# Attention pipeline of a transformer block: another order of the seven stages in a step, and squares before their sums

## The chip, the cores and the metric

The kernel runs on all eight cores of one Trainium2 chip. Each core works on one of the eight sequences, 2048 tokens by 1024 features, with the same program and all weights. The cores exchange nothing. The metric is device time in microseconds of the slowest core.

## The reference

Each sequence goes through a layer norm, and its result `xn` into two paths whose results are added to the input.

```python
xn = _layernorm(x)
x = x + attn_ref(xn) + ffn_ref(xn)

# attn_ref, for 2048 tokens
xi = rmsnorm(xn @ down_w + down_b, norm1_w)           # 1024 -> 512
o1 = branch(xi[..., :256], window=10, shift=5,  ...)  # 8 heads of 32
o2 = branch(xi[..., 256:], window=20, shift=10, ...)
x1 = xn + concat(o1, o2) @ up_w + up_b
out = x1 + gelu(rmsnorm(x1, norm2_w) @ ffn_w1 + ffn_b1) @ ffn_w2 + ffn_b2

# branch: q, k, v from xw @ qkv_w + qkv_b, inside each window
attn = softmax(q * scale @ k.T + bias + mask)
o = (attn @ v) @ pw + pb

# ffn_ref: 8 experts, the two best by a router are weighted in
w = softmax(top-2 logits of silu(t @ rw1 + rb1) @ rw2 + rb2)
y = t + sum_e w[e] * (silu(t @ ew1[e] + eb1[e]) @ ew2[e] + eb2[e])
```

## The kernel before

All is bf16 on TensorE with float32 sums. The program goes through its parts one after the other: layer norm and transposes of x (L304 to L365), the router (L372 to L483), attention (L486 to L857), the up projection with the dense feed-forward part (L859 to L1048), and the eight experts for all tokens (L1051 to L1147), which take the larger half of the time.

Operations are put down by `P.op(engine, builders, rd, wr)` (L50). Each engine gets its instructions in the order in which the calls are made, so the order of the calls is the order of every engine's queue. Dependences are kept by named resources: a reader waits for the writers of its resources, a writer for the earlier readers and also for the earlier writers, its own engine's among them. Two transposes into one PSUM bank by two calls thus run one after the other.

Attention begins with the down projection into XI (L556). Then, for each of four groups of 512 tokens, `xi_sq` (L570) squares the four chunks of XI on VectorE into SQ (L574) and sums each over the partitions by a matmul with ones into the bank PS (L578). ScalarE makes the inverse root of it (L582, L586), a matmul spreads it (L589), and `xi_norm` scales XI on VectorE (L596). SQ is one resource, `rSQ`.

For each of the two branches, queries and keys (L744) and values (L766) of all tokens are computed. Then 17 tiles of 120 tokens (12 windows of 10 or 6 of 20, with a bias tile that shuts out everything outside of a window) go through a software pipeline. `do_tile` (L617) gives seven stages for a tile:

- s0: TensorE, eight score matmuls (L629) into four banks of PF, heads h and h + 4 in one bank; VectorE adds the bias into Z (L635).
- s1: VectorE, negative maximum (L644), and its addition to Z (L649).
- s2: ScalarE, exponential from Z into E (L654).
- s3: VectorE, sum (L658), reciprocal (L661), and scaling of E (L666).
- s4: TensorE, eight transposes of E (L672) into a bank of PBF; ScalarE copies them into PTS (L677).
- s5: TensorE, eight matmuls with the values (L687), all into one bank; ScalarE copies two halves into AVS (L694).
- s6: TensorE, four matmuls of the projection (L705); ScalarE adds its bias into UPIN (L715) twice.

The loop at L791 runs over 23 steps. In step k, stage s of tile k - s is issued, so a step holds seven stages of seven different tiles; the first steps and the last have fewer. Z and E have four buffers, PBF, PTS and AVS two. The four score banks exist once, so s0 of a tile waits until L635 of the tile before has read them. The order within a step is written out: s4, s5, s6, s0, s1, s2, s3. A small tile of 10 tokens for the window at the end of the shifted sequence goes through the same stages without a pipeline (L850).

The loads of the weights of the dense part (L880, L882) wait for the end of attention.

Of the kernel before, what the change touches and what calls it, by code (L numbers as in the profile page):

```python
# [211 lines left out]
def build_nc():  # L212
# [276 lines left out]
    if True:  # L489
# [20 lines left out]
        SQ = esA.enter_context(nc.sbuf_tensor("SQ", [128, 4 * 512], BF16))  # L510
# [13 lines left out]
        if True:  # L524
# [24 lines left out]
            if True:  # L549
                rPA, rPB, rPC, rPS = rPF[0], rPF[1], rPF[2], rPF[3]  # L550
                pbanks = [(PA, rPA), (PB, rPB)]
                for nt in range(NNT):
                    for m in range(4):
                        ps, rps = pbanks[m % 2]
                        blds = [
                            (lambda m=m, nt=nt, k=k, ps=ps: t_.matmul(  # L556
                                ps[:, 0:512],
                                WDOWN[:, 512 * k + 128 * m: 512 * k + 128 * m + 128],
                                XN3[:, k, 512 * nt: 512 * nt + 512],
                                start=(k == 0), stop=(k == 7)))  # L560
                            for k in range(8)]
                        P.op("tensor", blds, rd=[rWDOWN, rXN4[nt]], wr=[rps])
                        P.op("scalar", (lambda m=m, nt=nt, ps=ps: s_.activation(
                            XI3[:, m, 512 * nt: 512 * nt + 512], ps[:, 0:512],
                            AF.Identity, bias=CS["dbc"][:, m: m + 1])),
                            rd=[rps, rCS["dbc"]], wr=[rXI])
                for c in range(4):
                    P.op("vector", (lambda c=c: v_.memset(XI3[:, c, 2048:2052], 0.0)),
                         wr=[rXI])
                def xi_sq(nt):  # L570
                    sl = 1024 * (nt % 2)
                    for c in range(4):
                        sq = SQ[:, sl + 512 * (c % 2): sl + 512 * (c % 2) + 512]
                        P.op("vector", (lambda c=c, nt=nt, sq=sq: v_.tensor_tensor(  # L574
                            sq, XI3[:, c, 512 * nt: 512 * nt + 512],
                            XI3[:, c, 512 * nt: 512 * nt + 512], ALU.mult)),
                            rd=[rXI], wr=[rSQ])
                        P.op("tensor", (lambda c=c, sq=sq: t_.matmul(  # L578
                            PS[0:1, 0:512], CS["onesb"][:, 0:1], sq,
                            start=(c == 0), stop=(c == 3))),  # L580
                            rd=[rSQ, rCS["onesb"]], wr=[rPS])
                    P.op("scalar", (lambda nt=nt: s_.activation(  # L582
                        RSTD[0:1, 0:512], PS[0:1, 0:512], AF.Ln,
                        bias=CS["epsc"][0:1, 1:2], scale=1.0 / 512)),
                        rd=[rPS, rCS["epsc"]], wr=[rRSTD])
                    P.op("scalar", (lambda: s_.activation(  # L586
                        RSTD[0:1, 0:512], RSTD[0:1, 0:512], AF.Exp, scale=-0.5)),
                        rd=[rRSTD], wr=[rRSTD])
                    P.op("tensor", (lambda: t_.matmul(  # L589
                        PC[:, 0:512], CS["onesf"][0:1, 0:128], RSTD[0:1, 0:512],  # L590
                        start=True, stop=True)),
                        rd=[rRSTD, rCS["onesf"]], wr=[rPC])

                def xi_norm(nt):
                    for c in range(4):
                        P.op("vector", (lambda c=c, nt=nt: v_.scalar_tensor_tensor(  # L596
                            XI3[:, c, 512 * nt: 512 * nt + 512], PC[:, 0:512],
                            CS["n1c"][:, c: c + 1],
                            XI3[:, c, 512 * nt: 512 * nt + 512], ALU.mult, ALU.mult)),
                            rd=[rPC, rCS["n1c"], rXI], wr=[rXI])  # L600

                for nt in range(NNT):
                    xi_sq(nt)
                    xi_norm(nt)
                P.replay(blk)
# [4 lines left out]
            if True:  # L610
# [112 lines left out]
                for br in range(2):  # L723
# [65 lines left out]
                                      WPJ, rWPJ, PBc, rPBc))  # L789
                    NSTG = 7  # L790
                    for step in range(17 + NSTG - 1):  # L791
                        for sidx in (4, 5, 6, 0, 1, 2, 3):
                            t = step - sidx
                            if 0 <= t < 17:
                                stages[t][sidx]()
# [381 lines left out]
```

How the kernel before makes its waits and increments, by code:

```python
            def body(eng, queue=list(queue), sems=sems):  # L111
                for waits, builders, semname, amt in queue:
                    for s, v in waits:
                        eng.wait_ge(sems[s], v)
                    for b in builders[:-1]:
                        b()
                    builders[-1]().then_inc(sems[semname], amt)
```

## Time and profile before

| what | value |
|---|---|
| runs | 3140.33 and 3503.17 us, median 3321.75 |
| the profiled execution | 3140.12 us |
| its span (first to last instruction, slowest core) | 3138.6 us |
| spans of the eight cores | 3126.6 to 3138.6 us |
| mean granted TensorE clock | 0.871 to 0.873 |
| TensorE busy | 2569.6 us, 82% |
| VectorE busy | 559.6 us, 18% |
| ScalarE busy | 632.4 us, 20% |
| GpSimd busy | 61.6 us, 2% |
| first L635 of branch one to the last of branch two | 305.6 to 827.7 us |

The span is what the trace covers; the device time has 1.5 us more. PE is TensorE, PEld its weight loads, DVE VectorE, ACT ScalarE, POOL GpSimd. An instruction's busy time runs from its start to its end, and the time in brackets behind a row is how long its engine stood idle before it, and which instruction ended that. The granted clock is a share of 2.4 GHz: 1.00 is the level of 2.4 GHz and 0.50 that of 1.2 GHz.

### The profile page before, as it was taken

How to read it: one execution, taken by the hardware profiler on the slowest of the kernel's cores; microseconds unless marked ns; L12 is line 12 of the kernel's file. 1: busy time of each engine (PE TensorE's matmuls, PEld its weight loads, DVE VectorE, ACT ScalarE, POOL GpSimd, SP SyncE). 2: the span in 40 equal slices, each digit the busy share in tenths (PEclk: the TensorE clock that was granted, in tenths of full speed). 3: DMA queues.
4: the chain of work that ended last, by engine and by line, in shares of the span. 5: the costliest groups of instructions: out<-in, count | busy, mean ns of one | idle time of the engine just before them, and what ended most of it. 6: DMA issues, size and time to landing. Idle time of an engine off the chain costs nothing.

```text
span 3138.6 us, 30438 instructions; the slowest of 8 cores (3126.6 to 3138.6 us)
## 1 busy us (share of the span) xinstructions
PE 2569.6 (82%) x11344; PEld 1119.3 (36%) x11344; DVE 559.6 (18%) x699; ACT 632.4 (20%) x1002; POOL 61.6 (2%) x80
## 2 busy tenths in 40 slices
PE   3764344533468969799999999999999999999999
PEld 1321122221223424334444444444444444444443
DVE  7013434233332130000010010100100001000000
ACT  2222112211211112111212112122121221211222
POOL 0000000000000000100000000000000000000000
PEclk9985555555568969899999999999999999999999
DMA  4220000000060000640420510600700700601201
GB/s 124 28 43 0 0 1 0 1 0 0 0 102 6 1 1 1 97 65 1 67 41 1 88 21 1 108 1 1 108 1 1 108 1 2 107 1 23 59 34 47
DMA packets 65621, 100.92 MB, mean 32 GB/s; under 512 B 4819, under 2 KB 40148, under 8 KB 65484
## 3 DMA queue, kind: packets, MB, share of 16 engines
q0 software_dynamic: 58080, 80.78, 16.9%
q1 hardware_dynamic: 7404, 18.20, 1.8%
q8 instruction: 100, 1.64, 0.2%
q14 instruction: 37, 0.30, 0.0%
HBM read 171.36 MB, written 8.39 MB: 57 GB/s over the span
## 4 chain that ended last, share of the span: by engine, by line
PE 80%; DVE 8%; issue 7%; DMA 2%; ACT 2%; SPq 0%; another core or an unknown queue 0%; DVEq 0%; POOL 0%; ACTq 0%; POOLq 0%
PE PF L1112 29%; PE PF L1093 27%; PE PF L1001 4%; PE PF L976 4%; PE PBF L672 3%; PE PF L687 2%; PE PF L381 2%; DMA WE<-e2w 1%; DVE Z L635 1%; PE PF L629 1%; DVE NEG L644 1%; DVE E L666 1%; PE PBF L918 1%; DVE SUMS L658 1%; PE PF L705 1%
## 5 line engine op out<-in xcount | busy, mean ns | idle before, releaser
L1112 PE MATMUL PF<-WE,EHS 128*128 128x512 bf16 x4096 | 918.6, 380 | 29.6 <-DMA WE<-e2w 10.6
L1093 PE MATMUL PF<-XN,WE 128*128 128x512 bf16 x4096 | 890.9, 379 | 14.4 <-DMA WE<-e1w 13.7
L1100 ACT ACTIVATE EHS<-PF,c_eb1c 128x512 bf16<-128x512 f32 x512 | 351.7, 687 | 1348.9 <-PE PF L1093 1348.7
L1112 PEld LDWEIGHTS PF<-WE,EHS 128*128 128x128 bf16 x4096 | 390.2, 98 | 545.5 <-issue 101.2
L1093 PEld LDWEIGHTS PF<-XN,WE 128*128 128x128 bf16 x4096 | 400.6, 98 | 499.1 <-issue 18.7
L1130 DVE SCALAR_TENSOR_TENSOR S<-PF,WTM,S 128x1024 bf16<-128x1024 f32 x128 | 164.3, 1284 | 1687.4 <-PE PF L1112 1468.5
L672 PE MATMUL PBF<-c_idb,E 120*120 120x120 bf16 (+1 forms) x288 | 90.8, 315 | 223.2 <-DVE E L666 185.6
L672 PEld LDWEIGHTS PBF<-c_idb,E 120*120 120x120 bf16 (+1 forms) x288 | 48.3, 168 | 265.0 <-issue 264.9
L976 PE MATMUL PF<-H,WF 128*128 128x512 bf16 x512 | 122.1, 404 | 6.7 <-ACT MID L983 6.7
L1001 PE MATMUL PF<-WF,MID 128*128 128x512 bf16 x512 | 116.0, 379 | 3.9 <-ACT MID L983 3.9
L687 PE MATMUL PF<-PTS,VT 120*32 120x120 bf16 x272 | 70.9, 260 | 35.7
L677 ACT COPY PTS<-PBF 120x960 bf16<-120x960 bf16 (+1 forms) x36 | 33.0, 917 | 295.8 <-PE PBF L672 295.8
L635 DVE TENSOR_TENSOR Z<-PF,c_bt 120x960 f32<-120x960 f32 x34 | 39.3, 1157 | 255.3 <-PE PF L629 255.3
L976 PEld LDWEIGHTS PF<-H,WF 128*128 128x128 bf16 x512 | 52.1, 103 | 78.2 <-issue 25.1
L342 PE MATMUL PBF<-c_idb,XNT 128*128 128x128 bf16 x128 | 33.8, 264 | 49.5 <-DVE XNT L333 32.8
L381 PE MATMUL PF<-XN,WR 128*128 128x512 bf16 x256 | 56.9, 385 | 20.8 <-DMA WR<-r1w 20.2
L983 ACT ACTIVATE MID<-PF,c_fb1c 128x512 bf16<-128x512 f32 x64 | 44.0, 687 | 133.3 <-PE PF L976 133.0
L1001 PEld LDWEIGHTS PF<-WF,MID 128*128 128x128 bf16 x512 | 47.5, 98 | 65.0 <-issue 12.1
L705 PE MATMUL PF<-AVS,WPJ 128*128 128x120 bf16 (+1 forms) x144 | 30.9, 264 | 42.8 <-ACT AVS L694 31.8
L1085 POOL DMA_DIRECT2D WE<-e2w x32 | 23.9, 756 | 1559.8 <-PE PF L1112 1559.7
L687 PEld LDWEIGHTS PF<-PTS,VT 120*32 120x32 bf16 x272 | 26.9, 99 | 77.2 <-issue 73.7
L629 PE MATMUL PF<-QKV 32*120 32x120 bf16 x272 | 37.5, 334 | 13.9 <-DVE Z L635 10.0
(129 smaller groups left out, 990.6 us busy)
## 6 DMA issues: line engine op xcount, KB each, us to landing
WE<-e1w POOLq DMA_DIRECT2D x32, 1024.0 KB, 38.8
WE<-e2w POOLq DMA_DIRECT2D x32, 1024.0 KB, 19.8
XST<-x SPq DMA_DIRECT2D x16, 512.0 KB, 3.5
out<-OST SPq DMA_DIRECT2D x16, 512.0 KB, 2.6
WF<-f1w POOLq DMA_DIRECT2D x1, 4096.0 KB, 30.4
WF<-f2w POOLq DMA_DIRECT2D x1, 4096.0 KB, 54.1
WR<-r1w POOLq DMA_DIRECT2D x1, 2048.0 KB, 17.5
WDOWN<-dw POOLq DMA_DIRECT2D x1, 1024.0 KB, 12.2
```

Source lines behind the costliest of these rows:

```text
L381: (lambda m=m, nt=nt, k=k, ps=ps: t_.matmul(ps[:, 0:512], WR1[:, 1024 * k + 128 * m: 1024 * k + 128 * m + 128], XN3[:, k, 512 * nt: 512 * ...
L629: P.op("tensor", (lambda h=h, a=a, b=b, nj=nj: t_.matmul(SCP[0:nj, 512 * a + 128 * b: 512 * a + 128 * b + nj], q_ap(h), k_ap(h), start=Tru ...
L635: v_.tensor_tensor(zsl, SCP4[0:nj, :, 0:2, 0:nj], bias_ap, ALU.add)),
L672: P.op("tensor", (lambda j=j: t_.transpose(PT[0:nj, 1024 * p2 + 128 * j: 1024 * p2 + 128 * j + nj], E[0:nj, 960 * p4 + nj * j: 960 * p4 + ...
L687: P.op("tensor", (lambda j=j, h=h, a=a, b=b: t_.matmul(PE2[32 * a: 32 * a + 32, 128 * b: 128 * b + nj], vdst[0:nj, 32 * h: 32 * h + 32], P ...
L705: t_.matmul(PE2[0:128, pcol: pcol + nj], WPJ[:, 256 * kc + 128 * mc: 256 * kc + 128 * mc + 128], AVS[:, 240 * p2 + nj * kc: 240 * p2 + nj ...
L976: (lambda m=m, k=k, ps=ps, hs=hs: t_.matmul(ps[:, 0:512], WF1[:, 2048 * k + 128 * m: 2048 * k + 128 * m + 128], H3[:, k, 512 * hs: 512 * h ...
L1001: blds.append(lambda k=k, h2=h2, tcl=tcl, ph=ph: t_.matmul(ph, MID3[:, k, 128 * tcl: 128 * tcl + 128], WF2[:, 1024 * k + 512 * h2: 1024 * ...
L1093: (lambda m=m, nt=nt, k=k, ps=ps, slot=slot: t_.matmul(ps[:, 0:512], WE13[slot][:, k, 128 * m: 128 * m + 128], XN3[:, k, 512 * nt: 512 * n ...
L1100: P.op("scalar", (lambda e=e, m=m, ps=ps: s_.activation(EHS3[:, m, 0:512], ps[:, 0:512], AF.Silu, bias=CS["eb1c"][:, 16 * e + m: 16 * e + ...
L1112: lambda k=k, h2=h2, tcl=tcl, e=e, PEx=PEx: t_.matmul(PEx[0:128, 512 * h2: 512 * h2 + 512], EHS3[:, k, 128 * tcl: 128 * tcl + 128], WE23[: ...
L1130: P.op("vector", (lambda e=e, tc=tc, PEx=PEx: v_.scalar_tensor_tensor(S[:, 1024 * tc: 1024 * tc + 1024], PEx[0:128, 0:1024], WTM[:, 8 * tc ...
```

## The change

Two places. In `xi_sq` the four squares of a token group get a quarter of SQ each, and all four are issued before the four sum matmuls; before, square and matmul were issued in turn, with two halves of SQ for each parity of the group. In the pipeline the seven stages of a step are issued as s0, s1, s2, s3, s4, s5, s6. No instruction is added or taken away, and none changes its shape.

```diff
                 def xi_sq(nt):
-                    sl = 1024 * (nt % 2)
                     for c in range(4):
-                        sq = SQ[:, sl + 512 * (c % 2): sl + 512 * (c % 2) + 512]
+                        sq = SQ[:, 512 * c: 512 * c + 512]
                         P.op("vector", (lambda c=c, nt=nt, sq=sq: v_.tensor_tensor(
                             sq, XI3[:, c, 512 * nt: 512 * nt + 512],
                             XI3[:, c, 512 * nt: 512 * nt + 512], ALU.mult)),
                             rd=[rXI], wr=[rSQ])
+                    for c in range(4):
+                        sq = SQ[:, 512 * c: 512 * c + 512]
                         P.op("tensor", (lambda c=c, sq=sq: t_.matmul(
                             PS[0:1, 0:512], CS["onesb"][:, 0:1], sq,
                             start=(c == 0), stop=(c == 3))),
@@
                     NSTG = 7
                     for step in range(17 + NSTG - 1):
-                        for sidx in (4, 5, 6, 0, 1, 2, 3):
+                        for sidx in range(NSTG):
                             t = step - sidx
                             if 0 <= t < 17:
                                 stages[t][sidx]()
```

## Rows read from the trace of the kernel before

**Rows 1.** Windows: stretch, its length, busy time (instructions) of each engine, clock, DMA
```profile
460.00:500.00 40.00, 17.06 (x70) 8.48 (x71) 12.76 (x13) 7.14 (x13) 0.00 (x0) 0.50 0.00 0
2000.00:3138.00 1138.00, 1120.86 (x5104) 490.51 (x5101) 102.70 (x80) 232.72 (x331) 22.44 (x28) 1.00 0.23 40
```

**Rows 2.** Waits, 470 to 523 us: total us, times, longest us
```profile
DVE Z L635 <- PE PF L629: 40.8, 4, 10.2
...
PE PBF L672 <- DVE E L666: 19.1, 3, 6.4
```

**Rows 3.** Timeline, one step of branch one: start us, us, instruction, idle before
```profile
471.41 1.16 DVE L635 TENSOR_TENSOR Z<-PF,c_bt 120x960 f32<-120x960 f32 x1 [10.21 <-PE PF L629]
...
473.73 1.16 DVE L649 TENSOR_TENSOR Z<-Z,NEG 120x960 f32<-120x960 f32 x1
...
476.36 1.16 DVE L666 TENSOR_TENSOR E<-E,RCPS 120x960 bf16<-120x960 bf16 x1
...
477.67 1.27 PE L672 MATMUL PBF<-c_idb,E 120*120 120x120 bf16 x3 [6.37 <-DVE E L666]
...
481.24 3.13 PE L687 MATMUL PF<-PTS,VT 120*32 120x120 bf16 x8
...
484.46 0.60 ACT L694 CAST AVS<-PF 128x120 bf16<-128x120 f32 x2 [2.10 <-PE PF L687]
...
486.42 1.20 PE L629 MATMUL PF<-QKV 32*120 32x120 bf16 x8
486.85 0.99 ACT L654 ACTIVATE E<-Z 120x960 bf16<-120x960 f32 x1
...
487.73 1.16 DVE L635 TENSOR_TENSOR Z<-PF,c_bt 120x960 f32<-120x960 f32 x1 [10.21 <-PE PF L629]
```

**Rows 4.** Timeline of VectorE: L635 of tiles 3 and 16, both branches
```profile
315.06 1.15 DVE L635 TENSOR_TENSOR Z<-PF,c_bt 120x960 f32<-120x960 f32 x1
...
520.38 1.16 DVE L635 TENSOR_TENSOR Z<-PF,c_bt 120x960 f32<-120x960 f32 x1 [10.22 <-PE PF L629]
...
622.32 1.15 DVE L635 TENSOR_TENSOR Z<-PF,c_bt 120x960 f32<-120x960 f32 x1
...
827.67 1.16 DVE L635 TENSOR_TENSOR Z<-PF,c_bt 120x960 f32<-120x960 f32 x1 [10.20 <-PE PF L629]
```

**Rows 5.** Timeline and one window of the tails (no s0 left), both branches
```profile
527.58 1.27 PE L672 MATMUL PBF<-c_idb,E 120*120 120x120 bf16 x3
...
527.66 1.16 DVE L649 TENSOR_TENSOR Z<-Z,NEG 120x960 f32<-120x960 f32 x1
...
850.26 1.17 PE L705 MATMUL PF<-AVS,WPJ 128*128 128x120 bf16 x4 [0.95 <-ACT AVS L694]
...
858.95 0.26 PE L705 MATMUL PF<-AVS,WPJ 128*128 128x120 bf16 x1 [0.95 <-ACT AVS L694]
...
857.00:861.00 4.00, 2.16 (x10) 0.98 (x9) 0.00 (x0) 1.24 (x4) 0.00 (x0) 0.50 0.00 0
```

**Rows 6.** Timeline: squares and their sum matmuls, in `xi_sq` and in `a4_sq`, `a4_stats`
```profile
242.97 0.42 DVE L574 TENSOR_TENSOR SQ<-XI 128x512 bf16<-128x512 bf16 x1
...
247.54 0.59 PE L578 MATMUL PF<-SQ,c_onesb 128*1 128x512 bf16 x1 [0.75 <-DVE SQ L574]
...
909.28 4.13 DVE L934 TENSOR_TENSOR H<-MID 128x512 bf16<-128x512 bf16 x8
...
921.97 2.05 PE L942 MATMUL PF<-H,c_onesb 128*1 128x512 bf16 x3
```

**Rows 7.** Timeline and windows: chained transposes at either level of the clock
```profile
909.32 3.34 PE L918 MATMUL PBF<-c_idb,MID 128*128 128x128 bf16 x10 [1.07 <-DVE MID L905]
...
928.15 1.09 PE L918 MATMUL PBF<-c_idb,MID 128*128 128x128 bf16 x3
...
908.00:912.00 4.00, 1.89 (x11) 0.81 (x9) 3.26 (x8) 0.00 (x0) 0.00 (x0) 0.96 1.01 163
...
928.00:932.00 4.00, 2.51 (x12) 1.08 (x11) 0.69 (x1) 1.68 (x3) 0.00 (x0) 0.50 1.08 174
```

## The prediction

> **What bounds the kernel now.** I read the windows by stage first. The expert layers fill TensorE (1120.86 of 1138 us in their last stretch, granted clock 1.00), and nothing in the change touches them. The attention stretch is different: in 40 us TensorE is busy 17.06, VectorE 12.76 and ScalarE 7.14, with the clock at 0.50, the 1.2 GHz level [rows 1]. No engine is full there, so the next view is the waits. In 53 us (a little over three steps of the tile pipeline) VectorE waits four times, up to 10.2 us each, for the score matmuls of L629, and TensorE waits three times, up to 6.4 us each, for the normalised exponentials of L666 [rows 2]. The two take turns.
>
> One step in order of time shows why [rows 3]. VectorE runs a step from the bias add L635 at 471.41 to the end of L666 at 476.36 + 1.16 = 477.52, 6.12 us with the handover. Only then may TensorE start the transposes (stage s4, 477.67), and behind them stand in its queue s5 (481.24), after ScalarE's copies at 484.46 s6, and last s0, the scores of the newest tile (486.42). VectorE's next step starts when these are there, at 487.73. The step is 6.11 + 10.21 = 16.32 us. The scores need nothing of what runs ahead of them: in the order written out at L792 they only stand behind it.
>
> **The change, part by part.** *The stage order.* No instruction is added or removed. On TensorE the same groups follow each other in a circle, but s0 of tile k moves ahead of s4 of tile k-4, which waits for VectorE's step k-1. So the scores for step k are computed while VectorE still works on step k-1, and two half-loops remain, each inside its own engine:
> - VectorE: 6.12 us a step.
> - TensorE: s4, s5, the ScalarE copies inside it, s6, then s0. The first three without any wait for VectorE are seen in the tail of the pipeline, where there is no s0: s6 starts at 850.26 and again at 858.95, 8.69 us [rows 5]. s0 takes 1.20 us (486.42) [rows 3]. Together 9.89 us.
>
> The longer loop sets the step: 9.89 instead of 16.32. The cost of s0 is the choice in it: 1.31 us is the most (until VectorE can start), and 0.14 more if s4 waits behind it as it does now for L666 (477.67 less 477.52); the least is about 0.9, if the next group starts before the last scores have ended. That makes a step 9.6 to 10.15 us; I take 9.89.
>
> Now the count, for a branch. The first four steps have no s4 to s6 and keep their order. L635 of tile 3 starts at 315.06 and of tile 16 at 520.38: 205.3 us; in the second branch 622.32 to 827.67, the same [rows 4]. After the change: steps 4 and 5 are VectorE's, 6.12 each. Tile 6 needs s4 and s5 ahead of its scores: 0.14 + 3.57 (477.67 to 481.24) + 3.13 + 1.31 = 8.15. Then ten steps at 9.89 are 98.9. Sum 119.3, a gain of 86.0. In the tail something is given back: now the s4 of step 17 starts 6.26 us after the last L635 (as 477.67 less 471.41 [rows 3]); after the change it stands behind the s4, s5, s6 of step 16, which run after the last scores, -1.31 + 1.20 + 8.69 = 8.58. The loss is 2.3, the net gain 83.7, for two branches 167.4 us.
>
> What is queued behind each moved instruction: s0 of tile k, now in front, waits for L635 of tile k-1 to have read the score banks. That read ends 1.16 us after VectorE's step k-1 has begun, and TensorE then has 8.69 us of s4 to s6 to do before it comes to this s0; it waits for nothing from step 6 on. s4 of tile k-4 needs L666 of step k-1: 6.12 + 0.14 + 0.11 us after the previous scores, against 9.89, so 3.5 us to spare. On ScalarE the exponential (s2) moves from the last place to the first. It needs the subtraction L649 of the step before, done at 473.73 + 1.16, which is 3.5 us after that step's L635 [rows 3], so it starts as soon as ScalarE is through with s6. It lasts 0.99 us and ends while TensorE is in its s0 and s4, before the copies of s4 and s5 are asked for. ScalarE is busy 7.14 us in 40 now [rows 1], so about 3 us a step, and has 9.9. The stages issue no DMA, and the SyncE and GpSimd queues aren't passed.
>
> *The squares (L573 to L581).* Now square and column-sum matmul alternate, because each square waits for the matmul before it: from the square at 242.97 to the end of the fourth matmul at 247.54 + 0.59 are 5.16 us. After the change four squares run in a row, and then four matmuls. Both kinds still run one behind the other: eight of the same squares elsewhere take 4.13 us, (4.13 - 0.42) / 7 = 0.53 from start to start, and three such matmuls 2.05 us, (2.05 - 0.59) / 2 = 0.73 [rows 6]. All four squares write one resource, so the first matmul waits for the last square: 3 x 0.53 + 0.42 + 0.15 + 3 x 0.73 + 0.59 = 4.94. The gain is 0.2 us a group, 0.9 in four; bounds are 0 (the first group runs partly at the higher clock now) and 2 (squares 0.42 apart). The round trip that goes away was no dearer than the two chains that come: it is cost moved from one place to the other.
>
> The sum is 167.4 + 0.9 = 168.3 us. The work behind attention (the weight loads of L880 and L882 are issued only when attention is through, then the expert layers) moves forward as a block. The span 3138.6 becomes 2970, and with the 1.5 us around it the profiled execution's 3140.1 becomes 2972. The median shown (3321.75) is the mean of 3140.33 and 3503.17; the sum goes by the first, which the profiled execution matches.
>
> **The rivals.** *The clock rises.* TensorE no longer stands still for 6.4 us in each step, so the 2.4 GHz level could be granted. For it: from 908 to 912, where a run of 512-column matmuls ends and transposes begin, the clock is 0.96 [rows 7]. Against it: the tail loop of s4 to s6 with no wait for VectorE, the nearest row to the new loop, stays at 0.50 [rows 5], and so do transposes without a gap [rows 7]. What it would give: chained transposes start (3.34 - 0.26) / 9 = 0.34 us apart at the higher clock and (1.09 - 0.26) / 2 = 0.415 at the lower [rows 7], 0.074 less. Sixteen chained matmuls in s4 and s5 make 1.2 us a step, over twenty full steps and the tails about 34 us: 2938 us. The Trainium skill, TensorE: Matmul & The Clock Gate, section on the HAM clock gate, holds that the engine is throttled by default and activity releases it; read simply, a loop without idle stretches should then reach the higher level, and its section on single matmul latency gives (219 + N) / 1.2 against (398 + N) / 2.4 ns, an estimate of 66 ns less for each chained matmul of 120 columns. By those the time would be about 4 us above this rival's. The tail loop doesn't bear out the first reading.
>
> *A hand-over to ScalarE grows.* If the exponential lands in front of the copies that s6 waits for (L694), it adds up to 0.99 us a step, over twenty steps 20 us: 2992. Against it stands the slack worked out above.
>
> *The loop stays tied.* If another buffer bound s0 of tile k to the end of s3, the step would remain near 16.3 and the time at 3140. The code shows no such resource: scores need the query and key rows, written before the pipeline, and the score banks, free after L635.
>
> *Slower.* VectorE's six operations now run beside TensorE in every step. If they stretched, so that its step became longer than 16.3 us (2.7 times), it would set a longer step than now; at 17 us the time is 3140 + 20 x 0.7 = 3154. Against it: L649 beside running transposes takes 1.16 us [rows 5], as it does alone at 473.73 [rows 3].
>
> **How the numbers follow.** The forecast of 2972 has 0.82; the higher clock 0.07; the dearer ScalarE hand-over 0.07; the tied loop 0.03; slower 0.01. The step's bounds (9.6 to 10.15) make 2966 to 2977. To the first rival below and the second above, with a little for their own sizes, the range is 2935 to 2995; it leaves out less than two in ten, as the sizes of the rivals are themselves uncertain. A measurement can tell about 2% (63 us) from no change. Forecast, clock and hand-over are all faster by more, 0.96; the tied loop is within 2% (0.03); slower 0.01.
>
> **What would show it.** Right: L635's starts are 9.6 to 10.2 us apart in steps 6 to 16 with VectorE's step still 6.1 us; TensorE's wait for L666 is gone from there and VectorE's wait for L629 is under 4 us; the tail steps are unchanged at 8.69; the clock in attention is 0.50; from the first square to the fourth sum matmul about 4.9 us; the expert stretch keeps its length. Wrong: a step above 10.5 with a wait of L694 or L687 for ScalarE (second rival); a clock above 0.6 in attention (first); matmuls of L629 that wait for L666 (third); VectorE operations much longer than 1.2 us (fourth).

## The result and the profile after

| | before | after |
|---|---|---|
| median of all runs | 3255.31 us (10 runs) | 2998.3 us (11 runs) |
| lowest run | 3140.33 us | 2969.3 us |
| the profiled execution | 3140.12 us | 2973.41 us |
| its span | 3138.6 us | 2971.9 us |
| mean granted TensorE clock | 0.871 to 0.873 | 0.892 to 0.895 |

The changed kernel is faster: ratio 0.9457, 95% interval 0.9407 to 0.9508. In some executions of either kernel the cores of one die show a lower TensorE clock than the others and take longer (up to 3506 us before, 3414 us after); the medians in the table contain these, while the ratios and the times of the experiments leave them out.

The expert layers are what they were: their last 1848 us hold the same 8224 weight loads in both traces. The 167 us come from attention, all but about 1 us of them from its pipeline. First one full step of it, from the timeline of the changed kernel (start us, us, engine, line, idle before); all lines behind L574 have one more than before (the squares have one less, L573). In the variants below the numbers shift by a few again, and the operation and its tiles tell which instruction it is.

```profile
383.63 0.77 PE L706 MATMUL PF<-AVS,WPJ 128*128 128x120 bf16 x3 [0.95 <-ACT AVS L695]
...
384.73 1.21 PE L630 MATMUL PF<-QKV 32*120 32x120 bf16 x8
385.16 0.99 ACT L655 ACTIVATE E<-Z 120x960 bf16<-120x960 f32 x1
...
385.87 0.83 PE L673 MATMUL PBF<-c_idb,E 120*120 120x120 bf16 x2
386.05 1.16 DVE L636 TENSOR_TENSOR Z<-PF,c_bt 120x960 f32<-120x960 f32 x1 [3.81 <-PE PF L630]
...
389.47 0.28 PE L688 MATMUL PF<-PTS,VT 120*32 120x120 bf16 x1
...
391.00 1.16 DVE L667 TENSOR_TENSOR E<-E,RCPS 120x960 bf16<-120x960 bf16 x1
...
394.65 1.21 PE L630 MATMUL PF<-QKV 32*120 32x120 bf16 x8
...
395.97 1.16 DVE L636 TENSOR_TENSOR Z<-PF,c_bt 120x960 f32<-120x960 f32 x1 [3.81 <-PE PF L630]
```

A step is 395.97 - 386.05 = 9.92 us; it was 16.32 [rows 3]. The transposes L673 start at 385.87, right behind the scores, where before TensorE stood idle 6.37 us ahead of them until L666 had ended. VectorE now begins its step while they run. It idles 3.81 us in a step instead of 10.21. TensorE no longer waits for VectorE: of its idle time of about 3.3 us a step, 0.95 us are spent on L695, and nearly all of the rest in gaps of about 0.15 us between its own matmuls.

The waits of the changed kernel from 380 to 433 us (total us, times, longest) say the same. The wait of the transposes for the exponentials is no longer in the list, and VectorE's wait for the scores is 3.9 us at most [rows 2].

```profile
ACT PTS L678 <- PE PBF L673: 20.9, 6, 3.5
DVE Z L636 <- PE PF L630: 19.1, 5, 3.9
```

The fill and the end of the pipeline, as starts of VectorE's bias add L636 for tiles 3, 4, 5, 6 and 16 of branch one, and the first transpose behind the last of them and that of the next step, which has no s0:

```profile
316.14 1.15 DVE L636 TENSOR_TENSOR Z<-PF,c_bt 120x960 f32<-120x960 f32 x1
...
322.15 1.15 DVE L636 TENSOR_TENSOR Z<-PF,c_bt 120x960 f32<-120x960 f32 x1
...
328.17 1.15 DVE L636 TENSOR_TENSOR Z<-PF,c_bt 120x960 f32<-120x960 f32 x1
...
336.37 1.16 DVE L636 TENSOR_TENSOR Z<-PF,c_bt 120x960 f32<-120x960 f32 x1 [2.09 <-PE PF L630]
...
435.77 1.16 DVE L636 TENSOR_TENSOR Z<-PF,c_bt 120x960 f32<-120x960 f32 x1 [3.87 <-PE PF L630]
...
444.31 0.32 PE L673 MATMUL PBF<-c_idb,E 120*120 120x120 bf16 x1
...
453.00 0.80 PE L673 MATMUL PBF<-c_idb,E 120*120 120x120 bf16 x2
```

Two steps of 6.0 us, one of 8.2, then ten that sum to 99.4: 119.6 us where there were 205.3 [rows 4].

The clock, by the window of 340 to 430 us in the changed kernel and that of 340 to 380 us in a variant of it (e8_grouped, below). Columns as in [rows 1].

```profile
340.00:430.00 90.00, 58.49 (x254) 29.50 (x253) 52.76 (x55) 28.41 (x55) 0.00 (x0) 0.50 0.00 1
```

```profile
340.00:380.00 40.00, 15.49 (x187) 11.14 (x188) 37.93 (x41) 19.58 (x39) 0.00 (x0) 0.50 0.00 1
```

TensorE is busy 65% of the time now. It was 43% in the window of [rows 1] and 40% over three whole steps (19.49 of 49 us, from 470 to 519 us). Its clock is still at the 1.2 GHz level, and so it is in the variant.

The squares, one token group from the timeline of the changed kernel:

```profile
245.27 2.01 DVE L573 TENSOR_TENSOR SQ<-XI 128x512 bf16<-128x512 bf16 x4
...
247.43 2.05 PE L579 MATMUL PF<-SQ,c_onesb 128*1 128x512 bf16 x3 [5.77 <-DVE SQ L573]
...
249.63 0.58 PE L579 MATMUL PF<-SQ,c_onesb 128*1 128x512 bf16 x1
```

From the first square to the end of the fourth sum are 249.63 + 0.58 - 245.27 = 4.94 us; they were 5.16 [rows 6].

### The profile page after: what moved, and what is told of

Same layout as the page of the kernel before. It is cut to its first block, busy times and chain, and to the rows that moved or that the text cites. A ratio compares the mean times of both kernels' runs of the same rounds, so it can differ in the third digit from the quotient of the medians.

```text
span 2971.9 us, 30248 instructions; the slowest of 8 cores (2961.3 to 2971.9 us)
## 1 busy us (share of the span) xinstructions
PE 2551.1 (86%) x11144; PEld 1118.4 (38%) x11344; DVE 559.1 (19%) x699; ACT 633.0 (21%) x1002; POOL 61.6 (2%) x80
## 4 chain that ended last, share of the span: by engine, by line
PE 83%; issue 7%; DVE 4%; DMA 2%; ACT 2%; another core or an unknown queue 0%; SPq 0%; DVEq 0%; POOL 0%; ACTq 0%; POOLq 0%
PE PF L1113 31%; PE PF L1094 29%; PE PF L1002 4%; PE PF L977 4%; PE PBF L673 3%; PE PF L688 3%; PE PF L381 2%; DMA WE<-e2w 1%; PE PBF L919 1%; PE PF L706 1%; PE PF L630 1%; PE PF L556 1%; DVE H L966 1%; PE PBF L342 1%; PE PF L897 1%
## 5 line engine op out<-in xcount | busy, mean ns | idle before, releaser
L673 PE MATMUL PBF<-c_idb,E 120*120 120x120 bf16 (+1 forms) x288 | 91.4, 317 | 52.8 <-DVE E L667 15.2
L673 PEld LDWEIGHTS PBF<-c_idb,E 120*120 120x120 bf16 (+1 forms) x288 | 48.3, 168 | 93.4 <-issue 90.8
L636 DVE TENSOR_TENSOR Z<-PF,c_bt 120x960 f32<-120x960 f32 x34 | 39.3, 1156 | 84.5 <-PE PF L630 84.5
```

The source lines that it names most:

```text
L673: P.op("tensor", (lambda j=j: t_.transpose(PT[0:nj, 1024 * p2 + 128 * j: 1024 * p2 + 128 * j + nj], E[0:nj, 960 * p4 + nj * j: 960 * p4 + ...
```

## The experiments

The theory to be tested: the step is the longer of two loops (TensorE 9.9 us, VectorE about 6) once s0 no longer stands behind the transposes, and was their sum before. Rivals: the place of ScalarE's exponential carries part of it; the squares do; VectorE is still on the path; TensorE's loop is bound by the matmuls themselves at the lower clock.

**Each part alone.** e1_order_only is the kernel before with the second half of the diff, e2_squares_only with the first half.

> Only the order of the stages changes; squares and sums stay as before. Theory (the order decouples VectorE from TensorE): the step of the 120-token tiles is 9.9 us instead of 16.3, device time about 2974 us, 0.9 us above the whole change, ratio 0.947. Rival (a good part of the gain comes from the squares, because their round trips cost more than the traces' steps say): 2980 us or more, ratio above 0.949.

Measured: 2972.55 us, ratio 0.9438 (0.9353 to 0.9523). The step is 396.70 - 386.79 = 9.91 us.

> Only the squares and their sums change; the order of the stages stays s4, s5, s6, s0, s1, s2, s3. Theory: a token group of this stage takes 12.22 us instead of 12.44, 0.2 us less, and the whole kernel stays at 3139 to 3140 us with steps of 16.3. Rival (as above): 5 us or more are gained in this stage.

Measured: 3137.6 us in one execution, where those of the kernel before beside it began at 3139.65; a token group takes 12.21 us (squares start at 243.47 and 255.68) and the step stays at 16.32. So the order is the whole gain that can be seen in the time. The squares' 0.2 us a group can be read in the trace alone.

**Which move of the order.** The order moves s0 ahead on TensorE, and s2 ahead on ScalarE. Two kernels on the base of the one before part them.

```diff
# e3_s0_first
-                        for sidx in (4, 5, 6, 0, 1, 2, 3):
+                        for sidx in (0, 4, 5, 6, 1, 2, 3):
# e4_exp_first
-                        for sidx in (4, 5, 6, 0, 1, 2, 3):
+                        for sidx in (2, 4, 5, 6, 0, 1, 3):
```

> Base is the kernel before, order s0, s4, s5, s6, s1, s2, s3: TensorE's queue as after the change, but ScalarE's exponential stays last in the step as before. Theory (the place of s0 in TensorE's queue is the whole gain): steps of 9.9 us, device time 2974 us, ratio 0.947. Rival (the gain also needs the exponential ahead of the copies, so that VectorE's sums find it in time): steps above 10.5 us, device time above 2986 us.

> Base is the kernel before, order s2, s4, s5, s6, s0, s1, s3: only ScalarE's exponential moves to the front, TensorE's queue stays as before. Theory: the step stays 16.3 us and the time 3140 us, since no chain runs through the exponential. Rival: if the exponential's place carries part of the gain, the step falls below 16 us.

Measured: 2971.74 us, ratio 0.9438 (0.9353 to 0.9523), for the first and 3140.74 us for the second. VectorE's timeline of e3_s0_first has

```profile
384.10 1.16 DVE L635 TENSOR_TENSOR Z<-PF,c_bt 120x960 f32<-120x960 f32 x1 [3.81 <-PE PF L629]
394.01 1.16 DVE L635 TENSOR_TENSOR Z<-PF,c_bt 120x960 f32<-120x960 f32 x1 [3.80 <-PE PF L629]
```

and that of e4_exp_first

```profile
373.32 1.16 DVE L635 TENSOR_TENSOR Z<-PF,c_bt 120x960 f32<-120x960 f32 x1 [10.20 <-PE PF L629]
...
389.65 1.16 DVE L635 TENSOR_TENSOR Z<-PF,c_bt 120x960 f32<-120x960 f32 x1 [10.21 <-PE PF L629]
```

Steps of 9.91 and 16.33 us. The place of s0 is the whole of it: with s0 in front the step is the same 9.91 us whether the exponential stands first or last, and with s0 behind it stays at 16.3.

**Is VectorE off the path, and from where is it on it again?** Extra additions into a tile that nobody reads stand at the head of s3, two or six of them; the outputs stay as they are.

```diff
                     def s3():
+                        for _ in range(2 if nj == 120 else 0):
+                            P.op("vector", (lambda: v_.tensor_tensor(
+                                PAD[0:120, 0:960], bias_ap, bias_ap, ALU.add)),
+                                rd=rd_bias, wr=[rPAD])
                         P.op("vector", (lambda: v_.reduce_sum(
```

> Base is the changed kernel. Two further VectorE additions of 120x960 into an unused tile stand at the head of s3 of every 120-token tile, ahead of L659, about 2.4 us a step. Theory (two loops side by side, VectorE with 3.8 us to spare in each full step): the step stays 9.9 us; only the two or three steps of the fill that VectorE sets grow, about 5 us a branch, 2983 us in all. Rival (VectorE is still on the path of each step): steps of 12.3 us and about 60 us more, 3035 us.

> Base is the kernel before, with the same two additions at the same place, ahead of L658. Theory (VectorE's six operations and TensorE's four groups stand one behind the other in each step): the additions cost in full, steps of 18.7 us, 14 steps a branch at 2.4, 3207 us. Rival (VectorE's 10.2 us of idle time in a step can take them): steps of 16.3 us and less than 10 us more.

> Base is the changed kernel, six such additions at the head of s3, about 7.4 us a step, which makes VectorE's step about 13.5 us. Theory (the step is the longer of two independent loops): steps of 13.5 us, VectorE without idle time in the full steps, and with fill and tail 65 us more a branch, about 3105 us, still below the kernel before. Rival (one chain through both engines remains): the step is 9.9 + 7.4 = 17.3 us and the time above 3170 us.

Measured: 2979.41, 3204.33 and 3102.71 us. The timeline of VectorE in e5_after_pad2, two steps:

```profile
389.42 1.16 DVE L638 TENSOR_TENSOR Z<-PF,c_bt 120x960 f32<-120x960 f32 x1 [1.48 <-PE PF L632]
392.82 2.41 DVE L662 TENSOR_TENSOR PAD<-c_bt 120x960 f32<-120x960 f32 x2
...
399.34 1.16 DVE L638 TENSOR_TENSOR Z<-PF,c_bt 120x960 f32<-120x960 f32 x1 [1.47 <-PE PF L632]
```

in e6_before_pad2:

```profile
384.51 1.16 DVE L637 TENSOR_TENSOR Z<-PF,c_bt 120x960 f32<-120x960 f32 x1 [10.21 <-PE PF L631]
387.90 2.41 DVE L661 TENSOR_TENSOR PAD<-c_bt 120x960 f32<-120x960 f32 x2
...
403.16 1.16 DVE L637 TENSOR_TENSOR Z<-PF,c_bt 120x960 f32<-120x960 f32 x1 [10.21 <-PE PF L631]
```

and in e7_after_pad6:

```profile
394.52 1.15 DVE L638 TENSOR_TENSOR Z<-PF,c_bt 120x960 f32<-120x960 f32 x1
397.91 7.46 DVE L662 TENSOR_TENSOR PAD<-c_bt 120x960 f32<-120x960 f32 x6
...
407.92 1.15 DVE L638 TENSOR_TENSOR Z<-PF,c_bt 120x960 f32<-120x960 f32 x1
```

The same 2.41 us leave the step at 9.92 in the changed kernel, where they only use up VectorE's idle time (3.81 to 1.48), and make it 18.65 in the kernel before, whose VectorE kept its 10.21 us of idle time in full. With 7.46 us more the step is 13.40, VectorE has no idle time, and TensorE waits 3.44 us in it for the scaling of E (L673 in this kernel). That is a maximum of two loops after the change, a sum before it. The 10 us of idle time that VectorE showed before were no reserve.

**What TensorE's loop is made of.** The theory says that most of it is TensorE waiting for its own matmul, since each `P.op` that writes a bank waits for the last one that wrote it. e8_grouped makes one operation of the eight matmuls of a stage, on the base of the changed kernel: such an operation waits once, at its first matmul, and signals once, at its last. The cut shows s4; s0, s5 and s6 are changed in the same way, s6 in pairs. e9_before_grouped does the same on the kernel before.

```diff
                     def s4():
-                        for j in range(8):
-                            P.op("tensor", (lambda j=j: t_.transpose(
+                        P.op("tensor", [(lambda j=j: t_.transpose(
                                 PT[0:nj, 1024 * p2 + 128 * j: 1024 * p2 + 128 * j + nj],
                                 E[0:nj, 960 * p4 + nj * j: 960 * p4 + nj * j + nj],
-                                CS["idb"][0:nj, 0:nj])),
+                                CS["idb"][0:nj, 0:nj])) for j in range(8)],
                                 rd=[rE[p4], rCS["idb"]], wr=[rPT[p2]])
...
```

> Base is the changed kernel. The eight matmuls of s0, of s4 and of s5 and the pairs of s6 are put down as one operation each, so TensorE no longer waits for its own matmul before the next into the same bank. Nothing is left out. Theory (TensorE's loop of 9.9 us sets the step, and most of it is that waiting): TensorE's loop falls to 5 to 6 us, VectorE's 6.1 us become the bound, steps of 6.1 to 6.3 us, the tail's steps near 5, and 90 to 125 us less in all: 2850 to 2885 us, ratio about 0.91. Rival (the matmuls themselves are the cost, since the clock is at its lower level): steps of 9 us or more and less than 25 us gained, 2950 us.

Measured: 2824.55 us, ratio 0.8997 (0.8979 to 0.9015), 25 us below the range expected. The timeline of TensorE and VectorE in one step of e8_grouped, and s6 in its tail:

```profile
348.99 1.15 DVE L634 TENSOR_TENSOR Z<-PF,c_bt 120x960 f32<-120x960 f32 x1
...
349.22 1.03 PE L670 MATMUL PBF<-c_idb,E 120*120 120x120 bf16 x8 [2.24 <-DVE E L665]
...
350.18 0.40 PE L682 MATMUL PF<-PTS,VT 120*32 120x120 bf16 x8
...
352.05 0.56 PE L700 MATMUL PF<-AVS,WPJ 128*128 128x120 bf16 x4 [1.47 <-ACT AVS L690]
...
352.54 0.46 PE L628 MATMUL PF<-QKV 32*120 32x120 bf16 x8
...
355.01 1.15 DVE L634 TENSOR_TENSOR Z<-PF,c_bt 120x960 f32<-120x960 f32 x1
...
405.19 0.56 PE L700 MATMUL PF<-AVS,WPJ 128*128 128x120 bf16 x4 [1.47 <-ACT AVS L690]
...
408.35 0.56 PE L700 MATMUL PF<-AVS,WPJ 128*128 128x120 bf16 x4 [1.47 <-ACT AVS L690]
```

The step is 6.02 us, VectorE's own, without a gap. TensorE's loop is 3.8 us (349.22 to 352.54 + 0.46), not the 5 to 6 that I had expected: the eight transposes take 1.03 us instead of 3.64, s5 0.40 instead of 3.13, s0 0.46 instead of 1.20, at the same clock of 0.50. So the matmuls themselves were the smaller part of the cost; the larger was that each waited for the one before and its signal. In the tail a step takes 3.16 us (s6 at 405.19 and 408.35), where I had put 5. That is most of the 25 us missing in the expectation: from tile 3 to tile 16 a branch takes 78.3 us instead of 119.6, 83 us in two branches, and of the remaining 66 us 51 lie between the last L635 of the pipeline and that of the small tile (54.21 us in branch one of the changed kernel and 28.57 in e8_grouped, 54.28 and 28.49 in branch two).

> Base is the kernel before (order s4, s5, s6, s0, s1, s2, s3), with the matmuls of s0, s4, s5 and s6 put down as in e8_grouped. Theory (in this order the two half-loops add up, whatever each takes): from the first transpose to the end of the scores TensorE takes 3.8 us in e8_grouped, so the step is 6.0 + 0.2 + 3.8 + 0.1 = 10.1 us, against 6.0 in the other order, and the time 2905 to 2930 us. Rival (once the waits for its own matmuls are gone the order no longer matters): steps near 6 and 2825 us.

Measured: steps of 10.17 us, as the timeline of VectorE on core 4 shows, with 4.05 us of its idle time in each:

```profile
374.64 1.16 DVE L633 TENSOR_TENSOR Z<-PF,c_bt 120x960 f32<-120x960 f32 x1 [4.05 <-PE PF L627]
384.81 1.16 DVE L633 TENSOR_TENSOR Z<-PF,c_bt 120x960 f32<-120x960 f32 x1 [4.05 <-PE PF L627]
```

The time was 2992.37 us, above the expectation, in an execution in which the clock was also lower in stretches without an edit (0.94 instead of 1.00 from 2000 to 2900 us, in the expert layers, on its slowest core, 6). So the kernel ran once more.

> The kernel of e9_before_grouped once more, for its time: in that run the steps were 10.17 us as expected, but the clock was at times lower than usual in stretches that the edit does not touch, on several cores, and the time was 2992 us. Theory (the steps set it): 21 full steps with 4.15 us more than in e8_grouped, so 2824.5 + 90 to 105 us, 2915 to 2930 us, ratio 0.93. Rival (the lower clock belongs to this kernel): 2940 us or more again.

Measured: 2930.65 and 2931.88 us, with steps of 10.17. That is a microsecond above the range, and it shows that the 2992 us weren't this kernel's own time. The order is worth 107 us even when TensorE's loop is short (2931 against 2824.5), and 100 of them lie between tile 3 and tile 16 of the two branches (128.1 us each instead of 78.3): the two loops add up in the one order, and the longer one counts in the other.

**The squares again.** In e10_squares_split, on the base of the changed kernel, each quarter of SQ is a resource of its own.

```diff
-                            rd=[rXI], wr=[rSQ])
+                            rd=[rXI], wr=[rSQ4[c]])
...
-                            rd=[rSQ, rCS["onesb"]], wr=[rPS])
+                            rd=[rSQ4[c], rCS["onesb"]], wr=[rPS])
```

> Base is the changed kernel. The four quarters of SQ become a resource each, so the sum matmul of a square waits for that square alone and runs beside the next square. Theory (after the change the two chains stand one behind the other because all four squares share one resource): from first square to last sum about 3.4 us instead of 4.9, 1.6 us less in each of four groups, 6 us in all: 2965 to 2968 us. Rival (the stage is bound by something else, the inverse root or the spread of it): the group stays at 12.2 us.

Measured: 2964.43 us. The timeline of one group in e10_squares_split:

```profile
244.56 1.43 DVE L573 TENSOR_TENSOR SQ<-XI 128x512 bf16<-128x512 bf16 x4
245.14 0.58 PE L579 MATMUL PF<-SQ,c_onesb 128*1 128x512 bf16 x1 [4.19 <-DVE SQ L573]
245.98 0.58 PE L579 MATMUL PF<-SQ,c_onesb 128*1 128x512 bf16 x1 [0.26 <-PE PF L579]
...
247.66 0.58 PE L579 MATMUL PF<-SQ,c_onesb 128*1 128x512 bf16 x1 [0.26 <-PE PF L579]
```

From the first square to the last sum are 3.7 us (to 247.66 + 0.58), a little more than the 3.4 expected, since the sums are 0.84 us apart instead of 0.73. A group takes 10.95 instead of 12.22, 5 us in four. The single resource had kept the two chains one behind the other.

**A version that is faster still.** e12_all is e8_grouped with the split squares and the same grouping for the transposes L917 and the sums L941.

> Base is e8_grouped, with the split squares of e10_squares_split and two more places put down as one operation each: the eight transposes of a 128-token tile (L917) and the eight sum matmuls (L941) ahead of the dense part. Theory (there too TensorE waits for its own matmul, 0.41 us a transpose and 0.73 a sum): from the first of these squares to the last sum a pair of groups takes about 18 us instead of 35, 30 to 40 us less for both pairs, and 6 for the squares: 2775 to 2795 us, ratio 0.886. Rival (VectorE or the bank hand-over bounds these places, as it bounds the step of e8_grouped): less than 15 us gained, 2810 us.

Measured: 2777.23 us, ratio 0.8845 (0.8825 to 0.8864). In a pair of token groups the stretch from the first square to the last sum takes 15.4 us; it took 35.5 before (909.28 [rows 6] to 944.19 + 0.58). The timeline of e12_all:

```profile
590.35 4.13 DVE L929 TENSOR_TENSOR H<-MID 128x512 bf16<-128x512 bf16 x8
...
590.39 1.05 PE L913 MATMUL PBF<-c_idb,MID 128*128 128x128 bf16 x16 [1.07 <-DVE MID L901]
...
603.81 1.89 PE L935 MATMUL PF<-H,c_onesb 128*1 128x512 bf16 x8
```

These 20 us need not all be the waits. In this stretch the clock was higher too: 0.89 from 590 to 606 us in e12_all, where e8_grouped has 0.55 from 595 to 612 us and 0.50 from 612 to 631. No run shows how the 20 us divide between the two. In the pipeline of e8_grouped that doubt doesn't arise, as the clock there was 0.50 in both kernels.

## Why the prediction was wrong in its range and right in its steps

It gave 2972 us and 2935 to 2995. The median measured is 2998.3, 3 us above the range, while the profiled execution took 2973.41 us. So the sum of the operations held, and the step that failed is the one from that sum to the number measured. The prediction says that "the sum goes by the first" of the two runs in view (3140.33, and not 3503.17), and it builds the range from the two rivals alone, 2992 "with a little for their own sizes" at the upper end. The spread between executions is no term of it: it was put at nothing without a reason, although the two runs lay 363 us apart.

What the runs showed in its place: of the eleven executions after the change, five lie between 2969.3 and 2973.41 us, five between 3052.05 and 3413.95, and the median is the single one between them. In that one, two cores ran at a mean clock of 0.883 and 0.885, the others at 0.892 to 0.896, and these two were the slowest (2996.8 and 2995.7 us against at most 2967.3). The term put at nothing thus measured 27 us at the median (2998.3 less 2971.2, the middle one of the five). That the miss was 3 us is chance: with one more execution like the first five in place of one of the last five, the median would have been 2973.4. A range for a median of such executions has to reach well above 2995. The forecast of a gain over 2% holds (ratio 0.9457), since the ratio compares like with like.

By its steps:
- *Two loops instead of a sum.* Right, and shown by e5, e6 and e7.
- *The step of 9.89.* 9.92. s0 was taken at 1.20 and s4 follows it without a gap (384.73 + 1.21 and 385.87). 8.69 in the tail is unchanged, from the s4 at 444.31 to the next at 453.00 in the changed kernel's timeline.
- *Steps 4 and 5 at 6.12, tile 6 at 8.15.* 6.01, 6.02 and 8.20. VectorE's step is 6.02 when it waits for nothing. The 6.12 was counted to the end of L666 (6.11, there is no hand-over in it), but the next L635 needn't wait for that end: L636 starts 0.09 us before it (322.15, where L667 ends at 321.08 + 1.16).
- *Tail give-back 2.3 us, s4 at 8.58 behind the last L635.* 8.54 (435.77 to 444.31).
- *Sum of 168.3 us.* From the first square to the first matmul of the up projection 658.9 us (230.72 to 889.63) have become 490.3 (233.03 to 723.33): 168.6. Of these the span shows 166.7: the profiled core after is another one, which reached its first square 2.3 us later and took 0.4 us less behind 723.33.
- *The squares, 0.9 us.* 5.16 to 4.94 in a group, exactly as worked out. The reason given (both chains still stand one behind the other, on one resource) is shown by e10.
- *The clock rises.* It didn't: 0.50 from 340 to 430 us. The tail loop was the right row to look at. So neither this rival's 0.074 us a matmul nor the 66 ns worked out from the Trainium skill was put to a test by any run here. A simple reading of the Trainium skill, TensorE: Matmul & The Clock Gate, section on the HAM clock gate, that activity releases the throttle, isn't borne out by this loop, in which TensorE is busy 65% and never idle for more than 1 us.
- *The dearer hand-over to ScalarE.* Not there: e3 and e4 show that the exponential's place is worth nothing, and the idle time before s6 is the same 0.95 us as before.
- *Tied loop; slower.* Neither. The step isn't near 16.3, and VectorE's additions and scalings last 1.16 us beside TensorE's work, as before.

The first square and the first matmul of the up projection, by which the sum was checked, before

```profile
230.72 0.43 DVE L574 TENSOR_TENSOR SQ<-XI 128x512 bf16<-128x512 bf16 x1
...
889.63 6.04 PE L896 MATMUL PF<-UPIN,WUP 128*128 128x512 bf16 x16 [0.92 <-ACT UPIN L715]
```

and after the change:

```profile
233.03 2.01 DVE L573 TENSOR_TENSOR SQ<-XI 128x512 bf16<-128x512 bf16 x4
...
723.33 5.88 PE L897 MATMUL PF<-UPIN,WUP 128*128 128x512 bf16 x15 [1.32 <-ACT UPIN L716]
```

What the prediction didn't ask is why TensorE's loop is 9.9 us long. The rows had it: chained transposes 0.41 us apart, with 0.26 us busy [rows 7]. It took the loop as given and only moved it; e8 shows that it was worth another 149 us (2973.41 to 2824.83 in the profiled executions).

## What to carry to other kernels

When two engines idle in turn, write down for each instruction in the queue whether it needs what the one ahead of it waits for. If it doesn't, put it ahead; the step then is the longer loop and not the sum, and the idle time of the other engine becomes a real reserve, which padding it on both kernels shows at once. Next look into the loop that is left: a dependence kept for a whole bank or buffer makes an engine wait for itself, and one operation for a group of matmuls took the 9.1 us of s0, s4, s5 and s6 (1.20 + 3.64 + 3.13 + 1.17) down to 2.5. Before giving a range for a median, look at the spread of the runs and not only at the profiled one.

## What the runs showed of the hardware

- Eight 120x120 transposes that each wait for the one before take 3.64 us, without those waits 1.03; eight matmuls of s5 take 3.13 and 0.40, both at a granted clock of 0.50.
- Sums that wait only for the sum before are 0.73 us apart. In e10_squares_split, where each also waits for its own square, they are 0.84 us apart, though the last square ended at 245.99 and the last two sums start at 246.82 and 247.66. A further wait that is already met thus seems to cost 0.11 us; no run changes that wait alone.
- A loop of small matmuls kept TensorE 65% busy for 90 us, never idle for more than 1 us, and the granted clock was 0.50, the 1.2 GHz level, throughout. The transposes and sums of 128 and 512 columns ahead of the dense part had 0.55 and 0.50 with the waits between them (e8_grouped), and 0.89 over 16 us without (e12_all).
